# A spectral layer and two convolutions on one core: image rows held as sums and differences of their halves

## The reference

```python
# layer 0: a 3x3 complex convolution in the Fourier domain
X = rfftn(x);  Yr = conv(Xr, wr) - conv(Xi, wi) + b_real;  Yi = conv(Xr, wi) + conv(Xi, wr) + b_imag
x = x + irfftn(Yr + 1j * Yi)                 # of _gn(x)
# layer 1: halves of the channels gate each other row by row
left = relu(sign(einsum('bkmd,bkd->bkm', u, v.sum(axis=2))))   # and right the same with u and v exchanged
x = x + concat([left * u, right * v])        # of _gn(x)
# layers 2 and 3: ordinary 3x3 convolutions, padding 1, 16 -> 16 channels
x = x + conv3x3(_gn(x), W2)
x = x + conv3x3(_gn(x), W3)
```

## Time and profile before

| | us |
|---|---|
| median of 3 runs | 4803.73 (4800.43 to 4807.34) |
| span of the profiled execution, the only time known of it | 4801.7 |
| PE busy | 4548.2 (95%) |
| DVE busy | 2925.9 (61%) |
| ACT busy | 2487.6 (52%) |
| layer-2 and layer-3 taps L1247 on PE | 1728.0 |
| Hilbert products L1165 on PE | 993.6 |
| mean granted clock of TensorE | 0.968 of full speed |

### The profile page before, as it was taken

One profiled execution on the slowest core, in us unless ns is written; L12 is line 12 of the kernel. 1 busy time (PEld: TensorE's weight loads), 2 busy tenths in 40 slices (PEclk: granted clock), 3 DMA queues, 4 the chain that ended last, 5 costly groups with the idle time before them and its releaser, 6 DMA issues.

```text
span 4801.7 us, 221653 instructions
## 1 busy us (share of the span) xinstructions
PE 4548.2 (95%) x84784; PEld 2936.4 (61%) x84784; DVE 2925.9 (61%) x10604; ACT 2487.6 (52%) x7085; POOL 3.2 (0%) x14
## 2 busy tenths in 40 slices
PE   4999999999999999999999999999999999998889
PEld 1555675556655566556665556655666557655566
DVE  1777717766277662777527765377744777257770
ACT  4455355544555445554455544555445554544435
POOL 0000000000000000000000000000000000000000
PEclk8999999999999899999999989999899999999999
DMA  7443015630166202662036510366004650034304
GB/s 196 111 124 100 4 29 172 176 102 4 47 177 176 79 3 61 178 177 63 4 86 177 176 41 3 105 176 174 24 3 120 177 163 19 3 111 122 90 4 143
DMA packets 290069, 468.11 MB, mean 97 GB/s; under 512 B 25392, under 2 KB 92144, under 8 KB 289264
## 3 DMA queue, kind: packets, MB, share of 16 engines
q1 hardware_dynamic: 289392, 458.29, 33.1%
HBM read 323.98 MB, written 134.22 MB: 95 GB/s over the span
## 4 chain that ended last, share of the span: by engine, by line
PE 91%; DVE 3%; issue 3%; DMA 1%; SPq 1%; ACT 1%; ACTq 0%; DVEq 0%
PE ps L1247 35%; PE ps L1165 19%; PE ps L1150 18%; PE ps L1158 6%; PE ps L1174 5%; PE ps L1024 5%; DMA x<-x 1%; PE ps L1273 1%; PE ps L1070 1%; PE ps L1071 0%; PE ps L1097 0%; PE ps L1305 0%; PE ps L1219 0%; SPq L360 0%; PE ps L1112 0%
## 5 line engine op out<-in xcount | busy, mean ns | idle before, releaser
L1247 PE MATMUL ps<-x,conv_s 32*32 32x512 f32 x49104 | 1728.0, 603 | 20.8 <-DVE x L948 16.7
L1247 PEld LDWEIGHTS ps<-x,conv_s 32*32 32x32 f32 x49104 | 1252.8, 103 | 437.9 <-issue 196.1
L563 ACT ACTIVATE x<-ps,vec 128x256 f32 (+1 forms) x1024 | 492.0, 495 | 1003.1 <-PE ps L1165 1003.1
L1165 PE MATMUL ps<-hil,shared 128*128 128x256 f32 x4096 | 993.6, 386 | 0.0
L814 DVE COPY vsb<-ps 128x512 f32<-128x512 f32 x512 | 329.9, 686 | 1043.6 <-PE ps L1150 1043.6
L1165 PEld LDWEIGHTS ps<-hil,shared 128*128 128x128 f32 x4096 | 740.2, 190 | 273.8 <-issue 194.1
L802 DVE SCALAR_TENSOR_TENSOR shared<-xin,trig 128x256 f32<-128x256 f32 x2048 | 821.6, 441 | 57.3
L629 ACT ACTIVATE x<-ps,vec 64x512 f32<-64x512 f32 (+1 forms) x768 | 527.2, 686 | 395.9 <-PE ps L1247 385.6
L1150 PE MATMUL ps<-shared 32*32 32x512 f32 x16384 | 656.4, 605 | 0.0
L620 ACT ACTIVATE x<-ps,vec 128x512 f32 x512 | 347.9, 685 | 439.6 <-PE ps L1247 439.6
L1150 PEld LDWEIGHTS ps<-shared 32*32 32x32 f32 x16384 | 306.2, 104 | 280.0 <-issue 216.8
(11 more groups left out here) (170 smaller groups left out, 2720.6 us busy)
## 6 DMA issues: line engine op xcount, KB each, us to landing
xin<-x SPq DMA_DIRECT2D x512, 256.0 KB
out<-x SPq DMA_DIRECT2D x512, 256.0 KB
shared<-x SPq DMA_DIRECT2D x448, 256.0 KB, 5.0
shared<-t_strip SPq DMA_DIRECT2D x512, 96.0 KB, 3.6
x<-x SPq DMA_DIRECT2D x64, 256.0 KB, 8.1
x<-t_proj SPq DMA_DIRECT2D x1, 2048.0 KB, 11.8
hil<-t_hil SPq DMA_DIRECT2D x1, 560.0 KB, 12.1
trig<-t_trig SPq DMA_DIRECT2D x1, 512.0 KB, 11.8
```

What stands on the lines that cost most here:

```text
L563: ins = nc.scalar.activation(split_in(strip_of(s))[:, q, :], split_in(ps[:, bank, :])[:, q, :], ACT.Identity, bias=v1(MEAN), accum_out=sum ...
L1165: mm = pe.matmul(split_in(ps[:, BY + 2 * odd + e, :])[:, int(q < 2), :], xt[:, e, q, :], hil[:, q, 0:HALF], start=False, stop=True, skip_g ...
L1247: mm = pe.matmul(ps[TM * cg:TM * cg + TM, banks[k], :], conv_s[TM * rg:TM * rg + TM, kw, second, :], x1[TM * rg:TM * rg + TM, of, kw:kw + ...
```

## The change

Each row is held as sum (plus) and difference (minus) of its two halves of 256 columns, from layer 0's input to the eviction of layer 3. The Hilbert transform of period 512 takes sums to sums and differences to differences, so that each of its four products has 128 result columns where it had 256. `x1` holds per strip two sides of 258 columns (256 and a pad either side), and the convolutions read both sides in one instruction. Layer 3's eviction turns sums and differences back into columns.

- `load_x` lands in `raw`, two slots, and waits for `x_taken`, which DVE raises when it has read a strip; a strip with e = 1 is loaded by two transfers, which exchange its halves of rows, so that layer 3's eviction need no longer exchange them for odd strips.
- `make_planes` reads `raw`, writes plus and minus to `xin`, and each plane in three instructions (two of 128 columns with a sum, one of 256); it works two pairs ahead, and the first two pairs of an image are made between the evictions of layer 3 of the image before (after pairs 20 and 22).
- `copy_v` of the second strip goes to ACT, ahead of the evictions in its queue. `evict` becomes three instructions.
- `gates` does four strips at a time, three instructions each, and then computes their pads; the memset on POOL goes. Layer 2's eviction is two instructions a strip, and ACT squares one strip of each pair, DVE the other.
- Layer 3: ACT evicts plus (one instruction a strip), DVE then makes both halves (two instructions a strip, from PSUM). DVE's `prepare` is cut into four parts between these evictions: after pairs 1, 3 and 6, and the first before them.

The diff, cut to its core:

```diff
-        hil_t[:, k, :HALF] = hil[rows][:, cols]
+        hil_t[:, k, :P] = hil[near][:, to] + sign * hil[far][:, to]
...
-                sp.wait_ge(mixed, i * PAIRS + pair - 1 + MIXED_CREDIT)
+                sp.wait_ge(x_taken, i * STRIPS + s + 1)
...
+                if e == 0:
+                    sp.dma_start(raw[:, 0, :], ...).then_inc(x_loaded[0], 16)
+                else:
+                    for h in range(2):
+                        sp.dma_start(raw[HP * h:HP * h + HP, 1, :], ...).then_inc(x_loaded[1], 16)
...
                     for q in range(2):
-                        ins = nc.scalar.activation(split_in(strip_of(s))[:, q, :], split_in(ps[:, bank, :])[:, q, :], ACT.Identity, bias=v1(MEAN), accum_out=...)
-                    ins.then_inc(y_evicted, 1)
+                        nc.scalar.activation(split_in(side_of(s, 0))[:, q, :], quarter(ps[:, bank, :], q, 0), ACT.Identity, bias=v1(MEAN2), accum_out=...)
+                    nc.scalar.activation(side_of(s, 1), ps[:, bank, HALF:N], ACT.Identity).then_inc(y_evicted, 1)
+                def copy_v(pair):
+                    act.wait_ge(mixed, i * PAIRS + pair + 1 + MIXED_CREDIT)
+                    act.wait_ge(turned, t0 + pair * 2 + T_CREDIT)
+                    nc.scalar.activation(vsb[:, 1, :], ps[:, BV + 1, :], ACT.Identity).then_inc(v_copied[1], 1)
...
+                    copy_v(t)
                     for e in range(2):
                         evict(t * 2 - 2 + e, ...)
                         turned_out(t * 2 + e, e)
...
-                        nc.scalar.activation(strip_of(s), ps[:, banks[k], :], ACT.Identity, bias=v1(MEANP), accum_out=...).then_inc(evicted, 1)
+                        nc.scalar.activation(side_of(s, 0), ps[:, banks[k], 0:HALF], ACT.Identity, bias=v1(MEANP), accum_out=...)
+                        nc.scalar.activation(side_of(s, 1), ps[:, banks[k], HALF:N], ACT.Identity).then_inc(evicted, 1)
+                    nc.scalar.activation(halves(zz[:]), both_of(s), ACT.Square, accum_out=cols[:, 3, ...]).then_inc(a2_squared, 1)
...
+                        nc.scalar.activation(x1[:, 2 * n + k, 0:HALF], ps[:, banks[k], 0:HALF], ACT.Identity, bias=v1(BIAS3), scale=0.5).then_inc(a_plus, 1)
...
+                    b.did(V.scalar_tensor_tensor(plus, raw[:, e, 0:HALF], v1(MEAN2), raw[:, e, HALF:N], ALU.subtract, ALU.add))
+                    V.tensor_tensor(minus, raw[:, e, 0:HALF], raw[:, e, HALF:N], ALU.subtract).then_inc(x_taken, 1)
...
+                            b.did(V.scalar_tensor_tensor(quarter(planes[:, a, k, :], q, 0), split_in(minus)[:, q, :], 1.0, ..., accum_out=...))
+                        ins = V.tensor_tensor(planes[:, a, k, HALF:N], plus, trig[:, a, 0:HALF], ALU.mult)
...
+                def step(pair, slot, dotting=True):
+                    copy_v(pair)
+                    make_planes(i, pair + 2, slot)
+                    if dotting:
+                        dots(pair - 2)
...
+                def evict3(n):
+                    for k, bank in enumerate(banks3(n)):
+                        dve.wait_ge(a_plus, t0 + s + 1)
+                        V.scalar_tensor_tensor(minus, ps[:, bank, HALF:N], -0.5, plus, ALU.mult, ALU.add)
+                        V.scalar_tensor_tensor(plus, ps[:, bank, HALF:N], 0.5, plus, ALU.mult, ALU.add).then_inc(evicted, 1)
+                for n in range(PAIRS):
+                    evict3(n)
+                    if more and n == 1:
+                        prepare_columns(i + 1, z)
...
+                    if more and n in PLANES_AT:
+                        make_planes(i + 1, pair, 2 * pair)
...
-                        mm = pe.matmul(split_in(ps[:, BY + 2 * odd + e, :])[:, int(q < 2), :], xt[:, e, q, :], hil[:, q, 0:HALF],
+                        mm = pe.matmul(quarter(ps[:, BY + 2 * odd + e, :], int(q < 2), q % 2), xt[:, e, q, :], hil[:, q, 0:P],
```

More of the change, by code:

```diff
@@ L77, in tables @@
     for k in range(4):
-        rows = split[k * P:(k + 1) * P]
-        cols = n[1::2] if k < 2 else n[::2]
-        hil_t[:, k, :HALF] = hil[rows][:, cols]
-        hil_t[:, k, HALF:] = g[rows]
+        par, sign = k // 2, 1 - 2 * (k % 2)
+        near, far = (np.arange(HALF * h + par, HALF * h + HALF, 2) for h in range(2))
+        to = np.arange(1 - par, HALF, 2)
+        hil_t[:, k, :P] = hil[near][:, to] + sign * hil[far][:, to]
+        hil_t[:, k, P:] = (g[near] + sign * g[far]) / 2
     mean_fix = np.zeros((P, NG))
@@ L389, in load_pair @@
                 for e in range(2):
-                    load_x(i, pair * 2 + e, pair, slot + e)
+                    load_x(i, pair * 2 + e, e)
                 for e in range(2):
@@ L832, in step @@
-                def step(pair, odd, uses, last=False, dotting=True):
-                    for e in range(2):
-                        if not last:
-                            s, k = pair * 2 + 2 + e, 2 * (1 - odd) + e
-                            b = steps_of(s)
-                            make_planes(b, s, k, u0 + uses + 1, pair + 1)
-                            assert b.n == DVE_B, b.n
-                        if e == 0:
-                            for f in range(2):
-                                copy_v(pair * 2 + f, f, pair)
+                        s = pair * 2 + e
@@ new lines, in dots @@
+                        late = type(s) is int and s >= STRIPS - 8
+                        dve.wait_ge(y_evicted, t0 + s + 1)
+                        dve.wait_ge(dotted, t0 + s - (not late) + DOT_CREDIT)
+                        V.scalar_tensor_tensor(halves(planes[:, 0, 0, :] if late else (vc, vy)[e]), both_of(s), 0.5, halves(colv), ALU.mult, ALU.mult,
+                                               accum_out=cols[:, 2, bass.ds(s, 1)]).then_inc(dotted, 1)
+                def step(pair, slot, dotting=True):
+                    copy_v(pair)
+                    make_planes(i, pair + 2, slot)
@@ L868, in image @@
                 ins.then_inc(f_ready, 1)
-                step(PAIRS - 1, 1, PAIRS // 2, last=True)
-                dots(PAIRS - 2)
-                dots(PAIRS - 1)
+                dots(PAIRS - 4)
+                copy_v(PAIRS - 1)
+                for pair in range(PAIRS - 3, PAIRS):
+                    dots(pair)
                 dve.wait_ge(dotted, t0 + STRIPS + DOT_CREDIT)
@@ L1246, in taps @@
                                 only = operands[1 - second] is None
-                                mm = pe.matmul(ps[TM * cg:TM * cg + TM, banks[k], :], conv_s[TM * rg:TM * rg + TM, kw, second, :],
-                                               x1[TM * rg:TM * rg + TM, of, kw:kw + N], start=(kw == 0 and (second == 0 or only)),
+                                mm = pe.matmul(halves(ps[TM * cg:TM * cg + TM, banks[k], :]), conv_s[TM * rg:TM * rg + TM, kw, second, :],
+                                               x1b[TM * rg:TM * rg + TM, of, :, kw:kw + HALF], start=(kw == 0 and (second == 0 or only)),
                                                stop=(second == 1 and kw == TAPS - 1), skip_group_check=True)
```

422 lines of the change are left out of this document (246 added, 176 removed).

## The result

The changed kernel takes **4721.48 us** (median of 4 runs, 4716.25 to 4725.96) against 4802.08 us in the same job: ratio 0.983, 95% interval 0.982 to 0.984. It is faster, as forecast, but by 81 us and not by 187. 4721 lies inside the wide range of 4540 to 4750 and outside the 4560 to 4685 of the forecast's own terms, and by the prediction's own sign, a step between 9.0 and 9.4 us, it falls in images 1 to 6. The profiled execution has a span of 4714.5 us, 87.2 less than before, at a granted clock of 0.959 (before 0.968).

What follows compares the result with a forecast made beforehand. PE bounds layer 0, then ACT before its second turn. Terms -242, -8, -14, +6, +63, +8, -6, +4 sum to -189: span 4801.7 to 4612.7 us, median 4615 (4560 to 4685; with two rivals 4540 to 4750).

Steps and rivals of the forecast that it cites:

- Part 3: Layer 0, DVE and the x loads at a 9.17 us step: covered but thin, late x costing 0.1 us at most.
- Part 1: Layer 0's Hilbert products: 128-column records at 118 ns, run of 8 in 0.94 us, 1.68 us less PE work a step.
- weight-load rival: Layer 0's Hilbert records: the 199 ns weight load sets them, 8 in 1.59 us, 4759 us; chance 0.06.
- Part 2: Layer 0: PE's second turn waits on ACT's evictions, 0.91 of 1.68 us is kept, step 9.17 us.
- The last image: Layer 0 of the last image, without projection: both evictions come earlier, about 1.45 us a step, -45 us.
- The first rival: Layer 0: DVE or the x loads set the step, 9.6 us, 4695 us in all; chance 0.20.
- the slower rival: Layer 0: the loop of raw slot, SP's order and DVE takes over; gain gone past 10.03 us steps; chance 0.09.
- The start of an image: Planes made two pairs ahead end the wait of `mix(1)`: -2 us an image, -14 us for seven.
- Parts 4 and 5: Layers 1 and 2: +6 us, PE waiting for four strips; layer 3: +63 stalls, +8 clock, -6 column sums.
- first stall: Layer 3: planes made after pair 20 delay DVE's eviction, PE stalls 4.6 us; after pair 22 another 3.5.

## Why the prediction was right in kind and wrong in size

The wait on ACT and the direction came as forecast; what failed is the price of the late loads, in Part 3, and a term that was put at nothing, the passage between images.

**Part 1, the record: right.** A run of 8 takes 1.00 us, inside the 0.95 to 1.06 that was named. The 199 ns of the weight-load rival were the distance from load to load and not a load's time, since 8 loads in 1.59 us keep the pace of the products that they wait for; one load takes a mean of 190 ns before and 193 after. These still lie beside records that follow each other at 125 ns. The rule of the Trainium skill (TensorE: Matmul & The Clock Gate, packing small matmuls), that loads in the same row group don't run beside a matmul, again does not describe this trace.

**Part 2, the wait on ACT: right**, as the timeline of image 0 shows term by term, and as the two runs show that lengthen and shorten ACT's chain. One term fits by luck: from the last record's start to ACT the rows of before give 0.7 us (1.6 to 2.31), the sum took 0.5 without saying why, and with 128 columns it is 0.44. The last image fell by 36.8 us where 45 and 2 were put: its steps are 8.8 to 8.9 against 8.75, and its first two are longer. There too the second turn waits on ACT, and `mix` on the evictions, as in the earlier trace rows:

```profile
4208.67 0.72 PE L1279 MATMUL ps<-eye,vsb 128*128 128x128 f32 x4 [0.71 <-ACT shared L577]
4209.94 1.15 PE L1255 MATMUL ps<-xin,shared 32*32 32x512 f32 x32 [0.56 <-ACT x L586]
```

**Part 3, the loads: the step that failed.** It said that the late x costs 0.1 us a step at most. Its parts were near: x issued 7.6 us after `mix` (1969.34 to 1976.78, 7.4), planes and dots 7.6 (1982.75 to 1990.43, 7.7), each strip 3.2 (3.25). Two things were wrong. From issue to DVE's start x takes a median of 5.4 us, 5.97 in the chain shown, where 5.0 to the landing were put after the earlier trace rows. And the sentence that ACT wouldn't let that turn start before 3.4 us after `mix` anyway, which made 1.4 us of cover: ACT holds the second turn. The first starts 1.98 after `mix` where DVE is in time (1991.58 to 1993.56 with the tables later).

What covers a late first turn is only that PE then waits less for ACT at the second: from turn to release it needs 8.96 us where image 0 has 9.31 or 9.45, so 0.35 to 0.5. Beyond that the lateness goes round: SP is released by a Hilbert run, and that run moves with the late turn. The prediction's 0.3 us of step for each microsecond is this loop of three steps; the working took the loop to be covered. At some 28.5 us it asks for 9.5 a step, more than the 9.22 that ACT leaves.

The first rival had a step of 9.6 for the loads, but its conditions didn't hold: planes took 6.46 us a pair (1982.75 to 1989.21) where it asked for 7.3, and x a median of 5.4 where it asked for 6.3. The mechanism, slot, SP's order and the table's wait, stands in the slower rival. Together they should have had the larger chance: in images 1 to 6 it is what happened (mean 9.57, some 75 us by 6 x 31 x 0.40 against 9.17; the run with the tables later gave back 55). The slower rival's threshold, 10.03, was passed by the run that put x first, by another wait: that of PE's projection for its loads.

**The start of an image: wrong.** -14 was put for planes that are ready sooner. It came in images 0 and 1 alone, where the first step fell from 11.2 to 7.8 us and from 12.1 to 9.3. In images 2 to 7 it is 11.2 to 12.4 us, no shorter than the 11.2 to 12.1 of before. The x of the third pair, which its planes need, stands in SP's queue behind the last stores of the image before (1263.16 and 1263.96 in the run with three loops written out, where the first steps are 11.4 to 12.1 too): the planes were put earlier, their loads were not. No run moves these loads, so that this cause is read from the rows and not tried. The passage had no term at all, +30: the working asked which work DVE would get in layer 3, not what stands behind its last piece.

**Parts 4 and 5.** Layers 1 and 2 came out near, +10 for +6; but layer 2 itself varies from some 105 to 111 us an image in every kernel here, with a granted clock of 0.94 in one of 111, so that such a sum tells little. Layer 3 has the forecast's first stall at its place, but of 3.4 to 3.7 us and not 4.6, and the second is 0 to 2.2 and not 3.5, in part since DVE's evictions follow each other at 0.33 us (1239.29 to 1239.62) and not at the 0.45 of the earlier trace rows: +44 for +65.

## What to carry to other kernels

When a wait is taken from the busiest engine, follow each transfer's issue round to itself (what releases the queue, what stands ahead of it, what its data release) over as many steps as it takes, and divide: a loop that is slower than the new step sets it, even where every engine in it has idle time, as here. An engine that is given the last work of a loop's body also brings its jump back to that place. And where a handshake sets the step, its own instructions can be worth their time one for one, as here; one run with a known delay shows it.

## What the runs showed of the hardware that was not expected

- A jump back of a loop over images shows as a gap without any instruction and without a wait. In the changed kernel it is 6.0 to 6.3 us on DVE in five passages and 8.9 in the first, and 5.5 from SP's last store to its next load, against 0.2 on SP when the loop is written out. It isn't a constant: without the two sums DVE's gap is 3.5 to 3.8. Of ACT's 4.53, some 2.4 are left when the loop is written out, as ACT then stands for `mix`.
- Splitting one 256-column eviction on ACT into 8 of 32 makes ACT's chain 0.42 us longer; 256 columns with a bias follow at 0.37 us, without at 0.26.
- Weight loads with a mean of 193 ns, one for each product record and all rows in use by both, lie beside records that follow each other at 125 ns: they overlap the products and one another.
